# State-space layer of a small language-model tower: the exponential of the softplus added by a DMA, and the front work put at other places

## The reference, cut to what matters

```python
xp, z = split(x @ W_in.T); xc = silu(conv1d(xp) + conv_b)          # 384 channels
dt, Bt, Ct = split(xc @ W_xproj.T, [12, 28])
dt = softplus(dt @ W_dt.T + b_dt)
h_t = exp(dt_t * A) * h_(t-1) + (dt_t * x_t) * B_t                 # 16 states per channel
y = sum over n of h_t[n] * C_t[n] + xc * D
out = (y * silu(z)) @ W_out.T                # 0.5 * (forward + backward) is added to x
```

## Time and profile before

| | |
|---|---|
| median of three executions | 4845.25 us |
| the profiled execution: time, span | 4843.86 us, 4842.1 us |
| mean granted TensorE clock | 0.960 |
| busy PE, DVE, POOL, ACT over the span | 90%, 70%, 66%, 49% |

### The profile page before, as it was taken

How to read it: one execution, slowest core, us unless ns; L and a number is a source line. 1 busy time by engine, 2 the same in 40 slices (tenths; PEclk the granted TensorE clock), 3 DMA queues, 4 the chain that set the end, 5 groups by cost and what they waited for, 6 DMA issues and landing times. The chain is left out here.

```text
span 4842.1 us, 62755 instructions
## 1 busy us (share of the span) xinstructions
PE 4357.8 (90%) x17088; PEld 2261.8 (47%) x17088; DVE 3396.1 (70%) x5016; ACT 2378.6 (49%) x4078; POOL 3186.6 (66%) x1637
## 2 busy tenths in 40 slices
PE   6999986997899999999999999999999975999994
PEld 4666654664333333343433334343333333666673
DVE  4766673111799999999999999999999985111114
ACT  2555542222566665656666565666656534221221
POOL 2222212441799999999999999999999961444441
PEclk9999997998899999999999999999999987999997
DMA  1000012342223232323233333223323221333456
GB/s 31 20 23 20 20 49 60 112 126 73 97 100 106 102 106 99 105 99 104 100 105 103 101 105 100 102 100 108 105 103 105 96 76 38 103 117 112 125 167 219
DMA packets 262442, 453.11 MB, mean 94 GB/s; under 512 B 38892, under 2 KB 175932, under 8 KB 262300
## 3 DMA queue, kind: packets, MB, share of 16 engines
q1 hardware_dynamic: 238876, 403.66, 25.5%
q0 software_dynamic: 23424, 48.00, 3.2%
HBM read 409.75 MB, written 41.81 MB: 93 GB/s over the span
## 5 line engine op out<-in xcount | busy, mean ns | idle before, releaser
L1745 POOL TENSOR_TENSOR m_xh<-m_u,m_Bb 128x1536 f32<-128x1536 f32 x512 | 1752.1, 3452 | 220.2 <-DVE m_u L1619 220.2
L1674 PE MATMUL bank<-m_xh,ident 128*128 128x512 f32 x3072 | 1442.7, 605 | 25.2 <-POOL m_xh L1734 25.2
L1701 ACT ACTIVATE bank<-m_dt,m_Ac 128x508 f32<-128x508 f32 x1536 | 1019.2, 683 | 419.3 <-DVE bank L1716 283.6
L1716 DVE TENSOR_TENSOR_SCAN bank<-bank,m_xh 128x512 f32<-128x512 f32 x864 | 1060.1, 1227 | 36.3 <-ACT bank L1701 7.8
L1674 PEld LDWEIGHTS bank<-m_xh,ident 128*128 128x128 f32 x3072 | 567.7, 191 | 804.9 <-issue 732.6
L1716 DVE TENSOR_TENSOR_SCAN m_xh<-bank,m_xh 128x512 f32<-128x512 f32 x672 | 774.2, 1204 | 31.6 <-ACT bank L1701 27.3
L1734 POOL TENSOR_TENSOR m_xh<-m_xh,m_Cb 128x1536 f32<-128x1536 f32 x224 | 773.1, 3452 | 11.7 <-DVE m_xh L1716 11.3
L1725 DVE TENSOR_TENSOR m_xh<-bank,m_Cb 128x512 f32<-128x512 f32 x864 | 597.7, 692 | 70.0 <-DMA m_Cb<-BC_rows 24.9
L1184 ACT ACTIVATE f1t_h<-bank,f1t_b 128x512 f32<-128x512 f32 (+1 forms) x276 | 147.9, 587 | 509.9 <-PE bank L1214 491.1
L1533 PE MATMUL bank<-m_xp,m_dg 128*128 128x512 f32 x768 | 349.8, 598 | 3.3 <-ACT m_xc L1541 2.6
L1114 POOL DMA_INDIRECT rows_y<-f1t_y,f1t_home x142 | 140.1, 987 | 317.4 <-DVE f1t_y L1155 288.1
(11 more groups left out here) (366 smaller groups left out, 6142.6 us busy)
## 6 DMA issues: line engine op xcount, KB each, us to landing
m_Bb<-BC_rows SPq DMA_DIRECT2D x256, 512.0 KB, 4.7
m_Cb<-BC_rows SPq DMA_DIRECT2D x256, 512.0 KB, 3.9
f1t_w<-f_w SPq DMA_DIRECT2D x46, 576.0 KB
f1t_w1a<-f_w SPq DMA_DIRECT2D x46, 384.0 KB
f0t_w<-f_w SPq DMA_DIRECT2D x22, 576.0 KB
f1c_yg<-rows_y SPq DMA_DIRECT2D x16, 768.0 KB, 8.2
f1t_w1b<-f_w SPq DMA_DIRECT2D x92, 96.0 KB
f0t_w1a<-f_w SPq DMA_DIRECT2D x22, 384.0 KB
```

Of the source, the lines that this page charges most:

```text
L1674: mm = pe.matmul(bank[:, c, :], K.ident[:, :], xh[n % NX][:, c, :], start=False, stop=(d == 1 and n == NS - 1))
L1701: act.activation(o[:, :, lo:hi], seqs(dt[d][:, c, :])[:, :, lo:hi], ACT.Exp, scale=Ac[:, c, n:n + 1]).then_inc(s_dA, 1)
L1716: dve.tensor_tensor_scan(o, bank[:, 3 + p % 3, way], xh[n % NX][:, c, way], 0.0, ALU.mult, ALU.add).then_inc(s_h, 1)
L1745: pool.tensor_tensor(xh[n % NX][:, :, :], u[d][:, :, :], Bb[q % RB][:, n % QN, :].unsqueeze(1).to_broadcast([P, DC, TOK]), ALU.mult).then_ ...
```

## The change

The adding of e is taken out of `pe_sp`. POOL issues a DMA, one position behind `act_e`, that adds e[d] to r in SBUF (768 KB); `pe_sp` then sums three tensors, with r last, and its first call waits for that DMA. `BY_POOL` becomes two sets of seven steps, one for each direction, with the counts and waits that follow from it. The gates of z come after dt in the front work of d = 1, and silu(z) moves to `act_xc` of the next slot. The waits of the shared bank 7 move with it, and nearly all positions of the table change. The core of the diff (left out are lines that only count reads by the new functions, and the same pick of `BY_POOL[d]` in the readers):

```diff
-            "y": (6, 9, 11), "pe_D0": (7, 11, 12), "pe_D1": (11, 23, 30), "pe_out": (17, 18), "out": (19, 22),
-            "act_rows": (11, 13), "rows": (12, 14), "stats": 14, "rstd": 17, "norm": 28, "pe_zT": (44, 47),
-            "act_zT": (45, 47), "pe_x0": (0, 1, 2), "act_x0": (1, 2, 5), "pe_conv0": (3, 5, 9), "act_conv0": (6, 9, 16),
-            "pe_conv1": (3, 6, 7), "act_conv1": (4, 6, 10), "pe_gate1": (10, 13, 16), "act_gate1": (13, 18, 20), "pe_dt0": (19, 22, 24),
-            "act_dt0": (22, 25, 27), "pe_dt1": (21, 25, 26), "act_dt1": (27, 28, 30), "pe_pj": (18, 20), "act_pj": (20, 25),
-            "act_xc": (19, 22), "act_e": (27, 32), "act_w1": (30, 34), "act_ln": (31, 35), "pe_sp0": (31, 36, 41),
-            "act_sp0": (36, 41, 42), "u0": (35, 39, 42), "pe_sp1": (38, 40, 42), "act_sp1": (39, 42, 43), "u1": (38, 40, 42),
+            "y": (6, 9, 10), "pe_D0": (12, 16, 17), "pe_D1": (5, 15, 21), "pe_out": (16, 17), "out": (13, 16),
+            "act_rows": (11, 13), "rows": (12, 14), "stats": 14, "rstd": 26, "norm": 36,
+            "pe_zT": (45, 47), "act_zT": (44, 46), "pe_x0": (0, 1, 2), "act_x0": (0, 1, 3), "pe_conv0": (3, 4, 5),
+            "act_conv0": (6, 9, 12), "pe_conv1": (1, 3, 4), "act_conv1": (2, 4, 8), "pe_gate1": (24, 26, 31), "act_gate1": (25, 28, 31),
+            "pe_dt0": (12, 15, 18), "act_dt0": (18, 21, 23), "pe_dt1": (20, 21, 22), "act_dt1": (19, 21, 22), "pe_pj": (10, 9),
+            "act_pj": (15, 12), "act_xc": (13, 8), "act_e": (23, 23), "act_w1": (26, 25), "act_ln": (27, 29),
+            "pe_sp0": (29, 35, 39), "act_sp0": (30, 38, 41), "u0": (30, 36, 40), "pe_sp1": (33, 36, 42), "act_sp1": (33, 37, 41),
+            "u1": (32, 37, 40),
-        BY_POOL = (0, 3, 4, 7, 10, 12, 15)
+        BY_POOL = (3, 4, 5, 10, 12, 13, 14), (0, 4, 6, 9, 10, 11, 14)
...
+        def act_gz(act, g):
+            act.wait_ge(s_zc, g * DC + DC)
+            act.activation(gz[:, :, :], gz[:, :, :], ACT.Silu).then_inc(s_gz, 1)
...  (act_xc)
-                if d == 1:
-                    act.wait_ge(s_zc, g * DC + DC)
-                    act.activation(gz[:, :, :], gz[:, :, :], ACT.Silu).then_inc(s_gz, 1)
+                if d == 0 and not first:
+                    act_gz(act, g - 1)
...
+            def pool_add(pool):
+                pool.wait_ge(s_e, s + 1)
+                stand_alone(pool, K.go)
+                pool.dma_start(r[:, :, :].rearrange("p c t -> p (c t)"), e[d][:, :, :].rearrange("p c t -> p (c t)"),
+                               accum_op=ALU.add).then_inc(s_er, 16)
+
             def pe_sp(pe, c):
                 if c == 0:
+                    if d == 1:
+                        pe.wait_ge(s_zc, g * DC + DC)
+                        stand_alone(pe, K.go)
                     pe.wait_ge(s_nc, s + 1)
                 elif not first:
                     pe.wait_ge(s_u, s * DC + c)
-                for k, t in enumerate((r, e[d], w1[d], lw)):
-                    mm = pe.matmul(bank[:, front(c), :], K.ident[:, :], t[:, c, :], start=(k == 0), stop=(k == 3))
+                for k, t in enumerate((w1[d], lw, r)):
+                    if c == 0 and t is r:
+                        pe.wait_ge(s_er, (s + 1) * 16)
+                        stand_alone(pe, K.go)
+                    mm = pe.matmul(bank[:, front(c), :], K.ident[:, :], t[:, c, :], start=(k == 0), stop=(k == 2))
...
+            put("pool", POS["act_e"][d] + 1, pool_add)
```

More of the change, by code:

```diff
@@ L1347, in mamba_phase @@
         POS = {
-            "y": (6, 9, 11), "pe_D0": (7, 11, 12), "pe_D1": (11, 23, 30), "pe_out": (17, 18), "out": (19, 22),
-            "act_rows": (11, 13), "rows": (12, 14), "stats": 14, "rstd": 17, "norm": 28, "pe_zT": (44, 47),
[3 rows of a table removed]
-            "act_xc": (19, 22), "act_e": (27, 32), "act_w1": (30, 34), "act_ln": (31, 35), "pe_sp0": (31, 36, 41),
-            "act_sp0": (36, 41, 42), "u0": (35, 39, 42), "pe_sp1": (38, 40, 42), "act_sp1": (39, 42, 43), "u1": (38, 40, 42),
+            "y": (6, 9, 10), "pe_D0": (12, 16, 17), "pe_D1": (5, 15, 21), "pe_out": (16, 17), "out": (13, 16),
+            "act_rows": (11, 13), "rows": (12, 14), "stats": 14, "rstd": 26, "norm": 36,
[3 rows of a table added]
+            "act_pj": (15, 12), "act_xc": (13, 8), "act_e": (23, 23), "act_w1": (26, 25), "act_ln": (27, 29),
+            "pe_sp0": (29, 35, 39), "act_sp0": (30, 38, 41), "u0": (30, 36, 40), "pe_sp1": (33, 36, 42), "act_sp1": (33, 37, 41),
+            "u1": (32, 37, 40),
         }
         NB = 7
-        BY_POOL = (0, 3, 4, 7, 10, 12, 15)
+        BY_POOL = (3, 4, 5, 10, 12, 13, 14), (0, 4, 6, 9, 10, 11, 14)
         ROWS_IN = 3
-        pool_reads = lambda n: sum(k < n for k in BY_POOL)
-        reads = lambda n: DC * (n - pool_reads(n))
-        READS, POOL_READS = reads(NS), pool_reads(NS)
+        of_pool = lambda d, n: sum(k < n for k in BY_POOL[d])
+        of_dve = lambda d, n: DC * (n - of_pool(d, n))
+        pool_reads = lambda g, d, n: g * (of_pool(0, NS) + of_pool(1, NS)) + d * of_pool(0, NS) + of_pool(d, n)
+        dve_reads = lambda g, d, n: g * (of_dve(0, NS) + of_dve(1, NS)) + d * of_dve(0, NS) + of_dve(d, n)
         of_q = lambda q: range(q * QN, (q + 1) * QN)
-        FIRST_POOL = [min((n % QN for n in of_q(q) if n in BY_POOL), default=None) for q in range(NQ)]
-        FIRST_DVE = [min((n % QN for n in of_q(q) if n not in BY_POOL), default=None) for q in range(NQ)]
+        first_pool = lambda d, q: min((n % QN for n in of_q(q) if n in BY_POOL[d]), default=None)
+        first_dve = lambda d, q: min((n % QN for n in of_q(q) if n not in BY_POOL[d]), default=None)
         PW = P + 2 * (TAPS - 1)
@@ L1399, in mamba_phase @@
         s_copied = sem("rows_in_psum")
+        s_er, = ctx.software(K, 1)
         s_gy, s_ops, s_out = sem("gated_ready"), sem("outps_ready"), sem("res_ready")
@@ L1442, in act_rows @@
                         stand_alone(act, K.go)
-                        act.wait_ge(s_prv, g * 2 * READS + reads(ROWS_IN))
+                        act.wait_ge(s_prv, dve_reads(g, 0, ROWS_IN))
                 else:
@@ L1510, in pe_gate @@
                 if c == 0:
-                    pe.wait_ge(s_cv, (s + 1) * DC)
+                    pe.wait_ge(s_abs, (s + 1) * 2 * DC)
                 else:
@@ L1552, in pe_proj @@
                 pe.wait_ge(s_xc, s + 1)
[L1553 to L1556, removed]
                 for c in range(DC):
@@ L1570, in pe_dt @@
                     pe.wait_ge(s_pj, s + 1)
+                    if d == 1 and deep:
+                        stand_alone(pe, K.go)
+                        pe.wait_ge(s_out, g * 2)
                 elif not first:
@@ L1669, in pe_sum @@
         def pe_sum(pe, g, d, n, c):
-            if n not in BY_POOL:
-                pe.wait_ge(s_prv, (g * 2 + d) * READS + reads(n) + c + 1)
+            if n not in BY_POOL[d]:
+                pe.wait_ge(s_prv, dve_reads(g, d, n) + c + 1)
             elif c == 0:
-                pe.wait_ge(s_prp, (g * 2 + d) * POOL_READS + pool_reads(n + 1))
+                pe.wait_ge(s_prp, pool_reads(g, d, n + 1))
             mm = pe.matmul(bank[:, c, :], K.ident[:, :], xh[n % NX][:, c, :], start=False, stop=(d == 1 and n == NS - 1))
@@ L1680, in pe_out @@
                 if not (isinstance(g, int) and g == NG - 1):
-                    pe.wait_ge(s_zc, (g + 2) * DC)
+                    pe.wait_ge(s_pj, g * 2 + 4)
             else:
@@ L1709, in dve_scan @@
             way = slice(None) if d == 0 else slice(None, None, -1)
-            if n in BY_POOL:
+            if n in BY_POOL[d]:
                 o = xh[n % NX][:, c, way]
@@ L1714, in dve_scan @@
                 if later(g, d) or p > 0:
-                    dve.wait_ge(s_prv, (g * 2 + d) * READS + reads(n) + c)
+                    dve.wait_ge(s_prv, dve_reads(g, d, n) + c)
             dve.tensor_tensor_scan(o, bank[:, 3 + p % 3, way], xh[n % NX][:, c, way], 0.0, ALU.mult, ALU.add).then_inc(s_h, 1)
@@ L1721, in dve_read @@
             q = n // QN
-            if c == 0 and n % QN == FIRST_DVE[q]:
+            if c == 0 and n % QN == first_dve(d, q):
                 dve.wait_ge(s_C[q % RC], (s * (NQ // RC) + q // RC + 1) * 16)
@@ L1729, in pool_read @@
             q = n // QN
-            if n % QN == FIRST_POOL[q]:
+            if n % QN == first_pool(d, q):
                 pool.wait_ge(s_C[q % RC], (s * (NQ // RC) + q // RC + 1) * 16)
@@ L1786, in sp_C_in @@
                 k = (q - RC + 1) * QN
-                sp.wait_ge(s_prv, s * READS + (reads(k) if k >= 0 else reads(k + NS) - READS))
+                of = (g, d, k) if k > 0 else (g, 0, k + NS) if d == 1 else (g - 1, 1, k + NS)
+                sp.wait_ge(s_prv, dve_reads(*of))
                 stand_alone(sp, K.go)
-                sp.wait_ge(s_prp, s * POOL_READS + (pool_reads(k) if k >= 0 else pool_reads(k + NS) - POOL_READS))
+                sp.wait_ge(s_prp, pool_reads(*of))
             sp_in(sp, Cb, s_C, NS, d, q)
@@ L1823, in program @@
             before(eng)
```

(9 more changed lines are left out.)

## The result

| | before | changed |
|---|---|---|
| median, us (20 runs each) | 4846.57 | 4837.18 |
| lowest to highest | 4837.85 to 4861.18 | 4825.58 to 4839.09 |
| profiled execution's span, us | 4842.1 | 4832.8 |

The ratio is 0.998, 95% interval 0.9974 to 0.9986. The change is 9 us faster, where 20 us were forecast. The first fence has the page's busy line and the median landing of DMAs, with the added one.

What follows compares the result with a forecast made beforehand. POOL and its wait for u were taken to set the 168.7 us group period. The larger of DVE's 167.3 and the ring's 167.4 us saves 1.3 us, over 15 groups -20 us, giving 4825 us; range 4780 to 4885.

Steps and rivals of the forecast that it cites:

- POOL's waits for u go, DVE becomes full: State-space stage: earlier u removes POOL's 9.5 us of waits per group; DVE, with 163.3 us of own work, is late next.
- the text's signs: Signs of being right: POOL's u waits under 6 us, PE's DMA waits backward only, backward u wait 0 to 2, period 167 to 168.
- L: Time from issue to landing of the adding DMA: taken as 7.0 us, between 4.9 and 17.4.
- The ring: Chain per group through POOL, adding DMA, PE, ACT and DVE: 159.2 us plus L, 167.4 with 1.2 of other waits.
- ACT's block: Table load, two silus, table load moved to backward position 13 among fast units: 1.7 us of DVE wait per group.
- Waits for u: DVE's waits for u, 1.7 us per group before, taken as 0.7 after the shorter PE sum.
- The copies of x: Start of the backward slot: copies at positions 0, 1, 3 among fast units cost DVE 1.1 us, an estimate.
- C rows: DVE's waits for m_Cb, 1.5 us per group before, taken as gone.
- DVE's floor with stalls: DVE's time per group: 163.3 us of own work plus waits of 1.7, 1.1 and 1.2, in all 167.3 us.
- the 99.4 us of DVE in the ring: DVE's part of that chain, from first backward u to end of step 12 in the next forward slot: 99.4 us.
- the tail: End of the stage, with no POOL read behind the last scan and a slower last step: nothing within 2 us, with the head.
- the collision's 4845: Rival: the added 768 KB run beside Bb and Cb and delay reads; no change, 4845 us, chance 0.10.

Runs made afterwards that it cites:

- the late DMA: The changed kernel with the adding DMA issued one POOL product later (3.4 us), behind dBx11; 4895.2 us, ratio to before 1.0084 to 1.0113.

## Why the prediction was wrong

*POOL's waits for u go, DVE becomes full:* right. They fell from 36 us in three groups to nothing. PE waits for the DMA in backward slots only and the first backward u by 0.53 us, as the text's signs had it; of its signs only the period failed, 169.0 for 167 to 168. The time DVE spends on its own work stayed at 169.0 - 5.5 = 163.5 us against the 163.3 of the text.

*L:* 7.0 forecast, 6.6 measured (median). The choice between 4.9 and 17.4 was made with a factor of 1.5 that no row gave, so that it came so near is partly luck. The issue costs POOL 0.82 us and is hidden, as said.

*The ring:* right in kind and nearly in size. The text's 159.2 plus the measured L of 6.6, the turn of 2.5 and 0.6 (the 1.2 at the second backward u in every second group) make 168.9 us; the trace has 169.0. It was just closed (0.53 us of wait), as the late DMA showed.

*ACT's block:* 1.7 forecast, 2.0 measured. *Waits for u:* 0.7 forecast, 20.0/15 = 1.3 measured; 0.6 of it follows the stretches of half clock, which the text did not reckon with. *The copies of x:* 1.1 forecast, no wait in the trace; the 0.5 for row copies neither. *C rows:* gone, as said.

*The failed step* is "DVE's floor with stalls: 163.3 + 1.7 + 1.1 + 1.2 = 167.3" and with it the 99.4 us of DVE in the ring. Both held a stall list without the turn of the loop, because the trace of before shows none. It was there, under six fast scans, and the new step sets uncovered it: 2.5 us in each of 13 turns, 32.7 us. With it the ring of the text goes from 167.4 to 169.9, and with L and the other waits in the ring as measured (0.4 and 0.6 less) to 168.9. So the steady part gained nothing where 20 us were forecast. A second term was mis-sized: the text put the tail at "nothing within 2 us", and it gave 8.0 us. That the kernel is faster at all is thus owed to the last group and the last sum, and not to the shorter period that was forecast; the direction came out right by luck. None of the cases named had this mechanism; the outcome lay between the forecast and the collision's 4845, and no collision is in the trace. The fit of the Trainium skill (DMA: Bandwidth & Descriptors, Anatomy of one DMA) gives, as an estimate, 3.8 us for such a DMA, 2.8 less than measured; the measurement decides.

## What to carry to other kernels

Where a loop turns, look at which work each engine has at that point. In these runs the turn showed in full between units whose second instruction waits for the first, and three scans that wait for no result of DVE hid it; that the difference lies in the queue is my reading, which no run separates from other differences of the two kinds of unit. Before changing which work stands at a loop's end, count the turn as a cost that may be hidden there now. After a stop of PE read its granted clock before calling a longer stretch a pause. And where an asynchronous transfer closes a ring through several engines, move its issue by one instruction each way before anything else.

## What the runs showed of the hardware

The turn of the loop costs DVE 2.5 to 2.7 us from the end of the last instruction to the start of the next (13 rows in the changed kernel, 33.1 us in 13 in the kernel before with slow units there), with loop bodies of one and of two groups. The Trainium skill, Runtime: NRT & Kernel Launch (Instruction fetch mechanics), says that a taken branch out of the fetched window has to load its target before execution goes on; these rows agree with that, though no run here separates the load from the rest of the turn. TensorE's granted clock stood at 0.50 for 3.4 us after PE had waited 2.06 us, and one product took 2.04 us in place of 1.10 after waits of 2.13 and 4.1 us; after other waits of 2.1 us it stayed at 1.00. An SBUF to SBUF addition by DMA of 768 KB landed in 6.5 to 10.9 us, with a median of 6.6, beside the row transfers, less than the 8.2 us of a plain load of that size from HBM rows.
